# Causal attention with one key head: transposed probabilities against a second, transposed score product

## The reference, cut to what matters

```python
x = layernorm(x)        # in the kernel; eps 1e-5
q = (x @ wq_w.T + wq_b).reshape(b, t, 32, 32)
k1, v1 = x @ wk_w.T + wk_b, x @ wv_w.T + wv_b         # one head of 32
scores = einsum('bqhd,bkd->bhqk', q, k1) / sqrt(32)
scores = where(causal, scores, -inf)
attn = einsum('bhqk,bkd->bqhd', softmax(scores), v1)
x = x + attn.reshape(b, t, 1024) @ wo_w.T + wo_b
```

## Time and profile before

| what | value |
|---|---|
| median of 3 runs | 3959.29 us (3958.81 to 3964.57) |
| profiled execution, its span | 3969.6 us |
| TensorE busy | 3404.7 us, 86% |
| VectorE, ScalarE, GpSimd busy | 2089.3, 1116.5, 618.2 us |
| a batch row of attention | 266.5 us |
| a steady head group | 24.0 us |

### The profile page before, as it was taken

How to read it: one execution, slowest core, us unless ns; L and a number is a source line. 1 busy time by engine, 2 the same in 40 slices (tenths; PEclk the granted TensorE clock), 3 DMA queues, 4 the chain that set the end, 5 groups by cost and what they waited for, 6 DMA issues and landing times. The chain is left out here.

```text
span 3969.6 us, 53353 instructions
## 1 busy us (share of the span) xinstructions
PE 3404.7 (86%) x20224; PEld 2841.5 (72%) x20224; DVE 2089.3 (53%) x3582; ACT 1116.5 (28%) x2964; POOL 618.2 (16%) x754
## 2 busy tenths in 40 slices
PE   1898998998989989989999778878787878787868
PEld 1786887887868878878788356757575757666656
DVE  3463663654636626546466236555565646464633
ACT  2341442423414414324244013121212121121221
POOL 0001001000010010000100033223232323232311
PEclk9999999999999999999999778888898988888878
DMA  6322222222222222132221400000101010101000
GB/s 213 96 75 94 79 63 96 78 70 89 75 83 75 67 93 84 60 101 79 73 75 46 154 22 22 13 31 11 33 9 34 6 38 6 37 3 41 1 21 22
DMA packets 105455, 234.99 MB, mean 59 GB/s; under 512 B 20170, under 2 KB 38858, under 8 KB 105202
## 3 DMA queue, kind: packets, MB, share of 16 engines
q1 hardware_dynamic: 100544, 228.22, 18.6%
q10 hardware_dynamic: 4658, 3.22, 0.3%
HBM read 139.10 MB, written 41.94 MB: 46 GB/s over the span
## 5 line engine op out<-in xcount | busy, mean ns | idle before, releaser
L305 ACT ACTIVATE probs<-ps_attn,neg_max 128x128 f32<-128x128 f32 (+3 forms) x1024 | 534.8, 526 | 1070.5 <-DVE neg_max L398 1045.5
L557 PE MATMUL ps_attn<-probs_t,v_pad 128*128 128x128 f32 x5120 | 696.3, 277 | 17.5 <-DVE probs_t L408 15.9
L557 PEld LDWEIGHTS ps_attn<-probs_t,v_pad 128*128 128x128 f32 x5120 | 626.7, 192 | 33.6 <-DVE probs_t L408 28.2
L398 DVE TENSOR_REDUCE neg_max<-ps_attn 128x1 f32<-128x384 f32 (+3 forms) x704 | 449.8, 639 | 315.9 <-PE ps_attn L526 313.7
L408 DVE COPY probs_t<-ps_attn 128x512 f32<-128x512 f32 (+1 forms) x704 | 447.1, 636 | 272.4 <-PE ps_attn L544 272.4
L1182 PE MATMUL ps_mixer<-m_w_hi,m_xt_hi 128*128 128x512 f32 x1024 | 429.0, 419 | 77.1 <-DVE m_xt_lo L1021 77.1
L524 PE MATMUL ps_attn<-k_stack,q_stack 96*128 96x128 f32 (+3 forms) x1024 | 371.1, 398 | 72.9 <-issue 50.6
L1183 PE MATMUL ps_mixer<-m_w_hi,m_xt_lo 128*128 128x512 f32 x1024 | 415.6, 406 | 0.0
L1184 PE MATMUL ps_mixer<-m_w_lo,m_xt_hi 128*128 128x512 f32 x1024 | 414.2, 405 | 0.0
L544 PE MATMUL ps_attn<-ident_sb,probs 128*128 128x128 f32 x2560 | 397.5, 274 | 0.0
L544 PEld LDWEIGHTS ps_attn<-ident_sb,probs 128*128 128x128 f32 x2560 | 285.2, 142 | 20.3
(11 more groups left out here) (189 smaller groups left out, 5408.3 us busy)
## 6 DMA issues: line engine op xcount, KB each, us to landing
wq_hi<-wq_split SPq DMA_DIRECT2D x64, 512.0 KB, 3.6
wq_lo<-wq_split SPq DMA_DIRECT2D x64, 512.0 KB, 4.5
q_stack<-q_hi SPq DMA_DIRECT2D x512, 64.0 KB, 2.0
x_ring<-in_a_x SPq DMA_DIRECT2D x32, 512.0 KB, 4.1
q_stack<-q_lo SPq DMA_DIRECT2D x256, 64.0 KB, 2.0
r_ring<-in_a_x SPq DMA_DIRECT2D x32, 512.0 KB, 3.7
x<-r_ring SPq DMA_DIRECT2D x32, 512.0 KB, 2.6
m_xs<-x SPq DMA_DIRECT2D x32, 512.0 KB
```

Source lines behind the costliest of these rows:

```text
L305: exp = nc.scalar.activation(probs[:, s % P_RING, m * n:(m + 1) * n], ps[:, s % S_RING, m * n:(m + 1) * n], ACT.Exp, bias=neg_max[:, s % S ...
L398: nc.vector.tensor_reduce(neg_max[:, s % STAT, 0:len(heads)], ps[:, s % S_RING, 0:n * len(heads)].rearrange("p (j k) -> p j k", k=n), AX.X ...
L557: mm = nc.tensor.matmul(ps[:, 6 + g % 2, i * P:(i + 1) * P], v_pad[:, k, lead:lead + P], probs_t[:, u % T_RING, cols], start=(j == 0 and k ...
```

## The change

The rows' blocks and barriers go: one block runs steps M = -2 to 64 over all 64 groups G of all rows. In step M, PE works on group M + 2's projection, M + 1's scores, M's turned scores and M - 1's values.

- Scores [query, key] serve the maximum alone. The mask is an fp32r product per unit, over all heads of the unit at once. DVE writes maxima to `top`, PE transposes it, ACT copies it (`copy_rows`), and SP's `shift` moves it as row 96 of `q_stack`, against a row of -1 in `k_stack`.
- Scores are made again as [key, query] (`turned_scores`), with the maximum subtracted in the product. ACT exponentiates them straight to SBUF, 11 instructions a group. GpSimd zeroes the upper triangle of the diagonal blocks (`cut`).
- Values, and denominators against a tile of ones, are full fp32 products with a 32-column stationary side, each head into its own 32 partitions of a bank (`weigh`). No transposes of probabilities, no spread of the inverse.
- DVE takes the reciprocal of the whole denominator bank, 128x512, and multiplies (`divide`). The low part of the result moves to POOL.
- x and the residual share one ring; the output product stands at the end of step M = 8, 16, ...

Cut to its core (helpers that only got row indices are left out):

```diff
-        q_stack = sb("q_stack", [KROWS, 2, GH, T], F32R)
-        k_stack = sb("k_stack", [KROWS, T], F32R)
-        v_pad = sb("v_pad", [P, TILES, 7 * HEAD])
+        q_stack = sb("q_stack", [KROWS + 1, 2, GH, T], F32R)
+        k_stack = sb("k_stack", [KROWS + 1, 2, T], F32R)
+        v_sb = sb("v_sb", [P, 2, TILES, HEAD])
+        ones = sb("ones", [P, HEAD])
...
+                def stack(G):
+                    sp.wait_ge(qhi_done, G + 1)
+                    if G >= 2:
+                        sp.wait_ge(st_ready, U * (G - 1))
...
+                def shift(G):
+                    sp.wait_ge(top_rows_done, G + 1)
+                    sp.dma_start(q_stack[KROWS:KROWS + 1, G % 2, :, :]...,
+                                 top_rows[:, :].bitcast(F32)).then_inc(top_in, DMA)
...
+                for M in STEPS:
+                    if inside(M):
+                        shift(M)
...
+                    if inside(M + 3):
+                        load_wq(M + 3)
...
+                    if inside(M + 2):
+                        stack(M + 2)
...
+                def cut(G, k):
+                    pool.wait_ge(exp_done, U * G + (4, 8, 10, 11)[k])
+                    diagonal = pt[k][:, :, 0:P]
+                    nc.gpsimd.affine_select(diagonal, diagonal, [[0, GH], [1, P]], ALU.is_ge, 0.0, base=0,
+                                            channel_multiplier=-1).then_inc(sel_done, 1)
...
+                def divide(G):
+                    dve.wait_ge(b_done, G + 1)
...
+                    nc.vector.reciprocal(att[:, :], ps[:, DEN, :]).then_inc(inv_done, 1)
+                    dve.wait_ge(inv_done, G + 1)
+                    nc.vector.tensor_tensor(att[:, :], ps[:, AV, :], att[:, :], ALU.mult).then_inc(att_done, 1)
...
+                def turned_scores(G, u):
...
+                    if u == 0:
+                        pe.wait_ge(top_in, (G + 1) * DMA)
+                    if n >= 2:
+                        pe.wait_ge(exp_done, n - 1)
+                    for m, j in enumerate(heads):
+                        mm = nc.tensor.matmul(ps[:, ST0 + n % 2, m * width:(m + 1) * width], k_stack[:, b % 2, k * P:(k + 1) * P],
+                                              q_stack[:, G % 2, j, k * P:T], start=(m == 0), stop=(m == len(heads) - 1))
+                    mm.then_inc(st_ready, 1)
...
+                def weigh(G, blocks, last):
+                    for k in blocks:
+                        for bank, side in ((AV, v_sb[:, (G // GROUPS) % 2, k, :]), (DEN, ones[:, :])):
+                            for j in range(GH):
+                                mm = nc.tensor.matmul(ps[j * HEAD:(j + 1) * HEAD, bank, k * P:T], side, pt[k][:, j, :],
+                                                      start=(k == 0), stop=(k == TILES - 1))
...
+                for M in STEPS:
+                    b = next_row(M)
+                    project = b is None and inside(M + 2)
+                    if project:
+                        q_part(M + 2, (0, 1, 2))
+                    if inside(M):
+                        tops_turned(M)
+                    if project:
+                        q_part(M + 2, (3,))
+                    if b is not None:
+                        transposes(b, 0)
+                    if inside(M + 1):
+                        scores(M + 1, 0)
+                        scores(M + 1, 1)
+                    if inside(M - 1):
+                        weigh_rest(M - 1)
+                    for u in range(U):
+                        if inside(M):
+                            turned_scores(M, u)
+                        if u + 2 < U and inside(M + 1):
+                            scores(M + 1, u + 2)
...
+                        if project and u in (1, 3, 4, 5):
+                            q_part(M + 2, ({1: 4, 3: 5, 4: 6, 5: 7}[u],))
+                        if u == 5 and inside(M):
+                            weigh_first(M)
...
+                    if b is not None:
+                        transposes(b, 3)
+                        kv(b)
+                        q_part(M + 2, range(CH))
+                        values(b)
+                    if (b := last_row(M)) is not None:
+                        output(b)
```

More of the change, by code:

```diff
@@ L22, in attention_program @@
     KROWS = 3 * HEAD
[L24 to L39, removed]
+    NG = BATCH * GROUPS
+    S_UNITS = [(3, (0,)), (3, (1,)), (3, (2,)), (3, (3,)), (2, (0,)), (2, (1,)), (2, (2,)), (2, (3,)), (1, (0, 1)), (1, (2, 3)),
+               (0, (0, 1, 2, 3))]
+    T_UNITS = [(0, (0,)), (0, (1,)), (0, (2,)), (0, (3,)), (1, (0,)), (1, (1,)), (1, (2,)), (1, (3,)), (2, (0, 1)), (2, (2, 3)),
+               (3, (0, 1, 2, 3))]
+    U, FIRST_B = len(S_UNITS), 4
+    S0, ST0, PROJ, AV, DEN, MISC = 0, 2, 4, 5, 6, 7
+    Y_TILES = 2 * TILES
+    DMA = 16
+    STACK = 3 * GH * DMA
     with ExitStack() as ctx:
@@ L55, in attention_program @@
         q_hi, q_lo = sb("q_hi", [P, T], F32R), sb("q_lo", [P, T], F32R)
-        q_stack = sb("q_stack", [KROWS, 2, GH, T], F32R)
-        k_stack = sb("k_stack", [KROWS, T], F32R)
-        v_pad = sb("v_pad", [P, TILES, 7 * HEAD])
[L59 to L64, removed]
+        q_stack = sb("q_stack", [KROWS + 1, 2, GH, T], F32R)
+        k_stack = sb("k_stack", [KROWS + 1, 2, T], F32R)
+        v_sb = sb("v_sb", [P, 2, TILES, HEAD])
+        ones = sb("ones", [P, HEAD])
+        pt = [sb(f"pt_{k}", [P, GH, T - k * P]) for k in range(TILES)]
+        top = sb("top", [P, P])
+        top_rows = sb("top_rows", [GH * TILES, P], F32R)
+        att = sb("att", [P, T])
         stats, mean_var = sb("stats", [P, 2, 2, 6]), sb("mean_var", [P, 2, 2])
@@ L138, in row_sem @@
[L138 to L146, removed]
@@ L595, in attention_program @@
-        row(None, 0)
-        with nc.Fori(0, BATCH - 1) as b:
-            row(b, b + 1)
-        row(BATCH - 1, None)
+        xr_in = [sem("xr_in_0"), sem("xr_in_1")]
+        stats_done, mv_done, eps_done, std_done, xn_done = (sem("stats_done"), sem("mv_done"), sem("eps_done"), sem("std_done"),
+                                                            sem("xn_done"))
+        xt_ready, xhi_done, xlo_done = sem("xt_ready"), sem("xhi_done"), sem("xlo_done")
+        kv_ready, kv_done, khi_done, k_done, vt_ready, v_done = (sem("kv_ready"), sem("kv_done"), sem("khi_done"), sem("k_done"),
+                                                                 sem("vt_ready"), sem("v_done"))
@@ new lines, in attention_program @@
+        wq_in, q_ready, qhi_done, qlo_done, qs_in = sem("wq_in"), sem("q_ready"), sem("qhi_done"), sem("qlo_done"), sem("qs_in")
+        s_ready, s_used, top_done, topt_ready, top_rows_done, top_in = (sem("s_ready"), sem("s_used"), sem("top_done"),
+                                                                        sem("topt_ready"), sem("top_rows_done"), sem("top_in"))
+        st_ready, exp_done, sel_done, a_done, b_done = (sem("st_ready"), sem("exp_done"), sem("sel_done"), sem("a_done"),
+                                                        sem("b_done"))
```

813 lines of the change are left out of this document (392 added, 421 removed).

## The result

The changed kernel takes **4267.34 us** (median of 4, 4256.95 to 4271.61) against 3961.93 us beside it (4 runs, 3958.81 to 3968.02): ratio **1.0759, 95% interval 1.074 to 1.0778**. The profiled execution's span is 4255.2 us.

The account below looks back on a forecast made before the run. TensorE was taken to bound steady groups, 24.0 us each. Start 146, 62 steps of 32.5, next-row extras 142, output extras 247 and end 81 sum to 2631 against 2218.5: +412 us, 4371 us; range 4055 to 4960.

Parts of the forecast that it names:

- the stack gap: Between turned scores and next scores: TensorE idles 6.3 us a step, waiting for twelve q_stack copies issued by SP.
- the divide gap: Before unit 4's scores: TensorE loses 2.6 us waiting for VectorE, whose maxima stand behind the reciprocal and product.
- the clock: TensorE after an idle gap: runs at 1.2 GHz for a while, costing 2.0 us per step.
- my own mechanism: Whole kernel: value passes two abreast, with the wait for q_stack; 4290 to 4470 us, chance 0.46.
- rival 2: Value products: passes of four strips stream at once, 4.3 us a group; kernel 4096 us, chance 0.18.
- Rival 1: Value products: strips do not overlap at all, 17.3 us a group; kernel 4921 us, chance 0.28.
- `weigh_rest`: Later part of a group's value and denominator products: 5.2 of their 8.6 us plus 0.2 of drain, 5.4.
- two abreast, not four: Value products: same-strip passes follow each other in program order, so only two heads overlap; 8.6 us a group.
- the 4.3 us end: Lower bound for a group's value products, with four heads' strips side by side; the other end was 17.3 us.
- next-row steps: Seven attention steps that also carry the next row's x: 20.3 us extra each, 142 in all.
- output steps: Seven steps that also carry the previous row's output product, covering the copies' wait: 35.3 us extra each, 247 in all.
- Rival 3: SP's q_stack copies: issued or landed fast enough that no wait arises, saving 8.3 us a step; 3915 us, chance 0.08.

Follow-up runs that it names:

- e2: The changed kernel with 24 useless products on TensorE ahead of the wait for q_stack: 4204.26 us, ratio 1.0593 to the kernel before.
- e7: The changed kernel with copies on two queues, projection chunks earlier, and scores waiting only for their own head's copies: 3743.64 us, ratio 0.9433 to the kernel before.
- e9: e7 with value and denominator products issued head by head instead of block by block: 4119.07 us, ratio 1.04 to the kernel before.
- e10: e7 with products issued bank by bank, then head by head, six passes in a row on one strip: 3934.13 us, ratio 0.9904 to the kernel before.
- e5: The changed kernel with the twelve q_stack copies on two queues, seven on SP and five on ACT's: 4062.9 us, ratio 1.0235 to the kernel before.
- e6: The changed kernel with copies on two queues and projection chunks earlier: 3897.86 us, ratio 0.9806 to the kernel before.
- e8: The changed kernel with only the wait changed, each head's scores waiting for its own three copies, all on SP: 3963.98 us, ratio 0.9981 to the kernel before.
- e1: The changed kernel with projection chunks moved ahead of the scores that wait for the divide: 4055.17 us, ratio 1.0218 to the kernel before.

## Why the prediction was right, and where not

The direction and its cause were right: the stack gap, the divide gap and the clock behind them, against a TensorE whose own work had shrunk. The size is in part luck: the values were put 4.1 us a step too high and the clock 2.4 too low, and the two errors offset each other. The measured time is below my own mechanism's 4290 to 4470 and above rival 2's 4096; the range of 4055 to 4960 holds it because it took in rivals 1 and 2. Of the 32.5 us of a step, terms against one measured (542.2 to 572.9):

| term | forecast | measured |
|---|---|---|
| last turned score to the landed stack | 9.2 | 9.3: 0.35 to the first issue, 6.89 to the last, 2.08 to the scores (gap 6.32 from start to start, 5.92 idle; forecast 6.3) |
| two score units | 0.7 | 1.5, at the lower clock |
| `weigh_rest` | 5.4 | 4.7 at the lower clock; 2.6 in e2, 3.1 in e7 |
| to unit 4's scores | 4.7 | 4.9 (divide gap 2.91 from start to start, 2.52 idle; forecast 2.6) |
| to `weigh_first` | 4.0 | 5.65, with 3.4 at the lower clock |
| `weigh_first` | 3.6 | 1.85 |
| units 6 to 10 | 2.9 | 2.9 |
| clock, apart | 2.0 | in the rows above, about 4.4 |
| sum | 32.5 | 30.7 |

The forecast's three terms of the first row, 0.2, 11 x 0.62 and 2.0, make 9.0 and not 9.2.

**The step that failed** is "beside the second pass of head j only the first of head j+1 can run: two abreast, not four". It rested on products starting in program order. They don't: e9 and e10 show that passes for different strips pass each other, and in the kernel's order, block by block over four heads, four run abreast. That makes the values 4.5 us at full clock (2.6 in e2 and 1.85 above), not 8.6. Rival 2, to which I gave 0.18, had this right, but at 4096 us it was too low by 171, most of it because it kept my 2.0 for the clock (2.4 a step, 149 in 62 steps). Eight 384-column passes take 0.64 us abreast (e7: 448.39 is where the next ones start, 447.75 where these do) and 8 x 0.322 = 2.58 serial (e9), a factor of 4.0. The Trainium skill ("TensorE: Matmul & The Clock Gate", Part 3) gives 2.38 for three column tiles, so the overlap that it states is borne out here. An estimate of the values from its figure is 17.3 / 2.38 = 7.3 us, or 5.5 if a fourth tile adds as much as the others; the forecast put that "near the 4.3 us end", which it is not. The same Part 3 of the Trainium skill states that matmuls start and end strictly in order; e10's starts contradict that for products on different strips, and the measurement decides.

**The term that was mis-sized** is the clock, 2.0 us. I counted one fall a step behind the stack gap and none behind the divide gap, although that one is of 2.5 us idle; two falls with 10.2 us at the lower level cost about 4.4 (0.7 + 2.0 + 1.7: each slowed part less its time in e2 or at full clock). Steps of one kernel with different times at the lower clock say the same: in e2, e5, e6 and e8 each 3.4 us more at the lower level goes with a step 1.2 to 2.0 us longer in the mean (groups of five steps or more). The earlier trace rows had only gaps of 4.7 us, and I took those for the shortest that matter. The reciprocal was 3.36 us instead of 2.97, where I had carried 5.5 ns an element from operands of 16 and 32 elements in SBUF to 512 out of PSUM; no run says whether the width or PSUM makes the difference.

**The stage.** The first full step ends at 150.1 (forecast 146). The 62 steps take 2286.6 us (2404): 62 x 1.6 less, next-row steps 16 extra instead of 20.3, output steps 36.9 instead of 35.3. (The next row's k, v and q products cover one stack gap, which I had left out; that alone is more than the 4.3.) The end takes 78 (81). Sum 2514.5 against 2631. The two profiled spans differ by 285.6 us: 294.9 more in attention, 9.3 less in the mixer. The medians differ by 305.

**The other rivals.** Rival 1 (serial strips) is what e9's order makes of blocks 1 to 3, and it would have cost 17.3 only without any overlap. Rival 3 (no stack gap) is false of the change as it stands. Its price of 8.3 us a step fits an ordinary step (e1 to e7, which takes the stack gap out: 27.3 to 19.2), but its break-even, 6.7 us saved in each of the 62 steps, was counted from a time 104 us too high: from the measured one it is 4.9 (305 / 62). e8 shows it: it takes 4.3 us of idle time out of the gap (5.92 to 0.25 and 1.33) and 37.4 us out of the row, 4.7 a step, and is at 0.9981. That it takes 6.5 us out of an ordinary step is near 6.7 by chance. With four abreast the rival gave 3640; e7, nearly free of both gaps, stands at 3744. GpSimd's cuts (0.66 us in the mean, 1.21 at most) were between my two bounds and hidden, as forecast.

**What stays open.** What exactly decides when the clock falls: in e2 it fell for 0, 3.4 or 6.8 us behind the same 2.5 us idle, in e8 it fell behind an idle time of 1.3 us, in e7, with 1.15 in the step shown, it fell in no ordinary step. No run isolates it. Also not tried: a third slot for `q_stack`, which would remove the wait, and fewer, larger copies.

## What to carry to other kernels

When a reordering reuses a slot later than before, count the DMA issues between "free" and "needed": twelve at 0.62 us made 7.5 us of a 30.7 us step, and the cure was not fewer bytes but a wait per consumer (303 us), a second queue (204 us) and independent work ahead of the wait instead of behind it (212 us). Price an idle gap on TensorE at its length and about half of the time that it then runs at the lower clock; a 2.7 us shorter instruction was worth 4.3 us. For products on column strips, issue round robin over the strips: the same 48 passes of blocks 1 to 3 took 3.1 us in that order, 6.1 with six passes on a strip in a row, and 9.3 with twelve.

## What was not expected of the hardware

- **Passes on different strips overtake each other, up to four per strip.** Four strips start 6 to 7 ns apart and run fully abreast (eight 384-column passes in 0.64 us, 2.58 one by one); a strip seems to take four passes (one running, three waiting), and a fifth holds up everything behind it. This was read from e9 and then forecast e10's head spacing (0.64 us, measured 0.675), duration (5.8, 6.1) and time (3910, 3934). The queue itself is inferred, not seen.
- **A full fp32 product's two passes do not keep other strips waiting**: at 512 columns four first passes start together, four second ones 0.45 us later, then a round every 0.43 us, as long as a single 512-column pass takes alone.
- **A reciprocal of 128x512 out of PSUM takes 3.36 us**, 6.6 ns an element, where a copy of the same shape takes 0.69. On the rows' 16 and 32 elements it was 243 and 331 ns.
- **Small copies on ACT's queue are no cheaper to issue**: 0.52 and 0.63 us singly and 3 in 2.36 us in e7, beside SP's 0.51 to 0.59 each.
